# Node-number lists stored as 8-bit instead of 32-bit integers in a graph-attention and tree-FFN kernel

## The reference

```python
x = x + gnn(layernorm(x), h_neigh, adj, ...)     # attention over 512 neighbours, 8 heads
x = x + ffn(layernorm(x)[None], w1s, b1s, w2s, b2s)[0]

def ffn(x, w1s, b1s, w2s, b2s):                   # DEPTH 7, 255 nodes
    current = 0 for every token
    for _ in range(8):                            # walk down the tree
        score = x . w1s[current] + b1s[current]
        current = current * 2 + (score > 0) + 1
    for the 8 nodes on the path:
        out += (x @ w2s[node] + b2s[node]) * gelu(|score|)
```

## Time and profile before

| what | us |
|---|---|
| median of 3 runs | 159.88 |
| the three runs | 159.72, 159.88, 160.49 |
| profiled execution's own time | 160.56 |
| its span, first to last instruction | 157.9 |
| outside the span in that execution | 2.66 |
| PE busy, DVE busy | 105.4, 109.5 |

### The profile page before, as it was taken

How to read it: one execution, slowest core, us unless ns; L and a number is a source line. 1 busy time by engine, 2 the same in 40 slices (tenths; PEclk the granted TensorE clock), 3 DMA queues, 4 the chain that set the end, 5 groups by cost and what they waited for, 6 DMA issues and landing times.

```text
span 157.9 us, 3163 instructions
## 1 busy us (share of the span) xinstructions
PE 105.4 (67%) x870; PEld 78.5 (50%) x871; DVE 109.5 (69%) x302; ACT 73.5 (47%) x174; POOL 40.1 (25%) x82
## 2 busy tenths in 40 slices
PE   0656008943878878776689759968988839769810
PEld 0143003733745555545346326447877829658810
DVE  0676935891699999997678899535635793785580
ACT  3141305890789989988407301444433322524320
POOL 2332850000000000000020002704536333674652
PEclk9999999997799999999999996999999995999995
DMA  4936840225999999999710000200000000000000
GB/s 144 293 128 158 173 116 14 57 83 150 393 407 401 457 452 415 399 460 437 311 44 28 0 0 0 53 18 0 0 4 0 0 2 0 0 33 0 0 17 17
DMA packets 6341, 22.35 MB, mean 142 GB/s; under 512 B 1755, under 2 KB 4826, under 8 KB 5722
## 3 DMA queue, kind: packets, MB, share of 16 engines
q1 hardware_dynamic: 4970, 20.78, 34.6%
q10 hardware_dynamic: 1104, 0.92, 2.0%
q0 software_dynamic: 256, 0.52, 1.1%
HBM read 20.91 MB, written 1.31 MB: 141 GB/s over the span
## 4 chain that ended last, share of the span: by engine, by line
PE 32%; DVE 19%; DMA 14%; issue 13%; ACT 8%; SPq 6%; POOL 3%; DVEq 3%; ACTq 0%; POOLq 0%
PE s_ps L660 10%; DMA early<-q_parts 7%; SPq L249 6%; PE turn_ps L523 4%; PE turn_ps L660 4%; ACT prob L391 4%; DVE prob L770 3%; DMA w_sb<-in_w_t 2%; PE aux_ps L660 2%; ACT prob_t L387 2%; POOL early L337 2%; DMA q_parts<-q_p 2%; PE misc_ps L660 2%; PE s_ps L492 2%; PE s_ps L502 2%
## 5 line engine op out<-in xcount | busy, mean ns | idle before, releaser
L523 PE MATMUL turn_ps<-ident,prob 128*128 128x128 f32 x128 | 23.0, 308 | 7.9 <-ACT prob L391 6.6
L391 ACT ACTIVATE prob<-prob,negmax 128x512 f32<-128x512 f32 x32 | 23.0, 720 | 9.6 <-DVE negmax L770 9.5
L349 POOL TENSOR_TENSOR early<-early,scaled_sb 128x128 f32<-128x128 f32 x48 | 20.5, 454 | 26.0 <-ACT scaled_sb L443 25.4
L777 DVE TENSOR_TENSOR prob_t<-turn_ps,prob_t 128x512 f16<-128x512 f32 x32 | 22.1, 689 | 6.2 <-ACT prob_t L387 6.2
L770 DVE CUSTOM_DVE_ANT_0 prob<-s_ps,mask 128x512 f32<-128x512 f32 x32 | 21.7, 682 | 6.5 <-PE s_ps L492 6.4
L660 PE MATMUL s_ps<-w,msg 128*128 x128 | 19.2, 295 | 7.9 <-issue 4.2
L523 PEld LDWEIGHTS turn_ps<-ident,prob 128*128 128x128 f32 x128 | 15.8, 155 | 16.3 <-ACT prob L391 15.5
L492 PE MATMUL s_ps<-early 96*128 96x512 bf16 x32 | 13.8, 437 | 13.2 <-DMA early<-q_parts 12.2
L660 PEld LDWEIGHTS s_ps<-w,msg 128*128 128x128 f32 x128 | 16.3, 200 | 10.4 <-issue 10.4
L387 ACT ACTIVATE prob_t<-turn_ps 128x512 f16<-128x512 f32 x32 | 18.6, 580 | 6.1 <-PE s_ps L502 5.6
L443 ACT ACTIVATE scaled_sb<-s_ps,coef 128x128 f32<-128x128 f32 x32 | 10.0, 363 | 20.8 <-PE s_ps L660 20.8
(11 more groups left out here) (150 smaller groups left out, 161.4 us busy)
## 6 DMA issues: line engine op xcount, KB each, us to landing
w<-in_w_t SPq DMA_DIRECT2D x3, 4096.0 KB, 22.9
w<-in_w_t SPq DMA_DIRECT2D x1, 4032.0 KB, 41.5
prob<-in_adj SPq DMA_DIRECT2D x1, 1024.0 KB, 9.8
k_parts<-early SPq DMA_DIRECT2D x1, 384.0 KB, 2.4
early<-k_parts SPq DMA_DIRECT2D x1, 384.0 KB, 4.6
q_parts<-q_p SPq DMA_DIRECT2D x1, 288.0 KB, 2.9
early<-q_parts SPq DMA_DIRECT2D x1, 288.0 KB
msg<-in_neigh_t SPq DMA_DIRECT2D x1, 256.0 KB, 2.9
```

The lines of the kernel that those rows point to most:

```text
L349: ins = nc.gpsimd.tensor_tensor(mine, mine, scaled_sb[:, i, :], ALU.add)
L391: nc.scalar.activation(prob[:, u % RING, :], prob[:, u % RING, :], ACT.Exp, bias=negmax[:, t, h:h + 1], scale=-1.0, accum_out=psums[:, t, ...
L523: last = nc.tensor.transpose(turn_ps[u % 2][:, m * P:(m + 1) * P], prob[:, u % RING, m * P:(m + 1) * P], ident[:])
L777: nc.vector.tensor_tensor(prob_t[:, v % 2, 1, :], turn_ps[v % 2][:], prob_t[:, v % 2, 0, :], ALU.subtract).then_inc(lo_moved, 1)
```

## The change

The view `nodes` is declared as unsigned 8-bit instead of 32-bit. The code of the loops is the same, and so are the order and number of the engines' instructions. With it change: the output type of the ACTIVATE on L424 (L425 after), the number of bytes that each `TENSOR_LOAD` on L64 covers (8 instead of 32), and the operations inside the `FUSED_REGOPS` that works out its address. The compiled programs hold these:

| stage | before | after |
|---|---|---|
| s = 0 | min, add -8, multiply by 4, add the base | min, add (base - 8) |
| s = 1, 2, 3 | min, subtract, add 256 s, multiply by 4, add the base | min, subtract, add (base + 256 s) |

`entries` and `token_s` stay 32-bit, and so the loads on L72 are the same.

```diff
+U8 = mybir.dt.uint8
...
-        nodes = view(row_pair[0:1], 0, TILES * NODES_PAD, I32, "p (a n) -> p (a n)", a=1)
+        nodes = view(row_pair[0:1], 0, TILES * NODES_PAD, U8, "p (a n) -> p (a n)", a=1)
```

## The result

The changed kernel takes 175.5 us (median of 4 runs, 175.15 to 175.63) against 159.8 us before (159.41 to 160.49): a ratio of 1.0974, 95% interval 1.0932 to 1.1016. It is 15.7 us slower; the forecast was 159.7, its range ended at 161.2. The profiled execution took 175.39 us. Runs more than 1.5% above the fastest of the same kernel, at a slower state, are left out of every ratio, and of the median and range beside it.

What follows compares the result with a forecast made beforehand. No engine's busy time decides; the chain of node-product turns from 105.4 us does, mostly through TensorE's load. Address arithmetic gains 184 ns, load and list write 0: 160.56 less 0.18 gives 160.38, against the median 159.7; range 158.5 to 161.2.

Steps and rivals of the forecast that it cites:

- Where it would be decided: Node products from 105.4 us: TensorE's load of eight list entries ends last, and TensorE idles 0.28 us for it.
- the ten turns: Of 16 node-product turns, those whose first TensorE product directly follows its load; nine paced by TensorE's load, one by VectorE's.
- The load itself: Time of each turn's list-entry load: taken to go by entries, eight before and after, so 0 change.
- the high end: List load if each entry is cut from a word by its own operation: 104 ns more on TensorE, 128 on VectorE.
- a trip for each entry: List load making a separate fixed trip per entry: 8 x 520 = 4.2 us a load, given almost nothing.
- nine turns and one: Count of node-product turns in which a load change shows: nine by TensorE's load, one by VectorE's.
- Address arithmetic: Two register operations fewer per turn: 26 ns on TensorE, 32 on VectorE; 184 ns gained, bounds 150 and 266.
- The gain factor of 0.65: Share of a TensorE turn's gain that counts, because the chain VectorE - TensorE over two turns is about equally long.
- The write of the lists: ScalarE's ACTIVATE writing the lists: output width makes no difference, priced at 0; without cover 0.1 us would show once.
- A: Rival, faster: list loads get cheaper by bytes, 0.8 us less, 159.1; with full effect 158.6; chance 0.22.
- B: Rival, slower: entries are cut out of words in the list load, 0.8 us more, 160.7; chance 0.16.
- C: Rival, clock: TensorE's clock falls a second time, products of that stretch take some 1.7 us longer, 161.4; chance 0.03.

Runs made afterwards that it cites:

- experiments 3 to 6: Kernel before, lists written as 32-bit and as bytes: all load 32-bit (control) 161.38 us; bytes loaded by TensorE alone 174.73, VectorE alone 168.29, ScalarE alone 165.77.
- experiment 11: Kernel before plus a second 32-bit list for TensorE, node numbers times 128, saving a multiplication in each product's address: ratio 1.0006 (0.997 to 1.0041).

## Why the prediction was wrong

- **Where it would be decided: right.** TensorE's load ends last in a turn, what is added to it counts nearly in full (11.7 us in the ten turns, of 13.2), and it weighs more than VectorE's, as experiments 3 to 6 show.
- **"The load itself": this step failed.** I took 0 and put the high end at 104 ns for TensorE; it measured 1329. I did name "a trip for each entry", but at 4.2 us a load, and gave it almost nothing, since "eight entries cost no more than 72 ns over four now". That comparison was unsound twice. The four-entry rows were each sequencer's first load: a second one of four takes 345 ns on TensorE, and eight take 592, so four more cost 247, not 72. And I took that difference for a price by entries or bytes, where it is one trip of four. At 247 ns a trip, eight trips would be 1.98 us, an estimate from those rows; the load measured 1.92.
- **How the loss counts.** My rule of nine turns and one gives 9 x 1.33 + 1.23 = 13.2 us. The ten turns grew by 11.7. The rule left out the loads that had been hidden: 2.7 us came from the two turns under the bias products and 1.3 from the first load, under the transposes; the three turns around the sums gave back 0.7. That makes 15.0 in the loop, and the loop began 0.7 us later.
- **Address arithmetic.** The operations went as said, for 18 to 19 ns instead of 26. That was the whole gain, and it is lost in the rest.
- **The gain factor of 0.65** found no support. By it experiment 11 would gain 10 x 72 ns x 0.65 = 0.47 us, ratio 0.997, which lies at the very edge of its interval; the ten turns of its trace gained 0.02 us. It is probably too high, but one execution of each doesn't settle it.
- **The write of the lists:** 0. The ACTIVATE took the same 1.01 us.
- **Rivals.** A, where a load gets cheaper with fewer bytes, went the wrong way: bytes do not enter (1921 ns for eight of them in the loop, 1922 for sixteen). A boundary of 16 bytes does appear in the loads here, 0.53 us for eight 32-bit entries that start on it and 1.68 four bytes off it, but eight bytes from the same start took 1.67 us too. The runs show about 0.2 us an entry as soon as the group trip is lost (1672 ns for eight bytes on SyncE), and less than that for whole groups (980 ns for sixteen entries). B had the right sign and about a twentieth of the size. C did not cost: the low clock moved, and the load covered it.

## What to carry to other kernels

Before a narrower type is put where a sequencer loads registers, ask whether the load stays a whole number of packed, 16-byte aligned groups of four 32-bit entries; here it made 592 ns into 1921 and the kernel 10% slower to save bytes that nobody waited for. A price read off two rows must not include a sequencer's first load, and a difference between two sizes says little of the form in between. When the trace holds no row for the new form and the instruction is on the path of every turn, the far bound has to be priced with a real chance, or the range is too narrow.

## What the runs showed of the hardware

- Loading registers from SBUF on SyncE: 0.28 us for one 32-bit entry, 0.31 for four packed and aligned ones, 0.53 for eight, 0.75 for twelve, 0.98 for sixteen; entries over a full group cost 0.18 to 0.24 each. With 8 or 16 bits, gaps, or a start 4 or 8 bytes off: about 0.2 us an entry, 1.67 for eight.
- A sequencer's first load of four entries took 0.18 us (TensorE) to 0.25 us (VectorE) more than its second, and SyncE's first of eight 0.21 us more than a later one.
- A modulo by a constant, or a right shift by 16, in a fused register instruction on TensorE cost 38 ns, a multiplication 9 by the one comparison made.
- ScalarE wrote 1x1024 entries in 1.01 us as 32-bit and as 8-bit.
